# A gated cross-attention kernel of two layers: work moved across the layer boundary, Wffn's maximum in the third pass, O's scaling elsewhere in eight units

## What is computed

```python
x = x + tanh(g_xattn[0]) * L0_xattn(layernorm(x), ctx, Wq, Wk, Wv, Wo, q_norm_w, k_norm_w)   # 32 heads, 8 kv heads of 128, q and k rms-normed
x = x + tanh(g_ffn[0])   * L0_ffn(layernorm(x), weight)
x = x + tanh(g_xattn[1]) * L1_xattn(layernorm(x), ctx, Wq, Wk, Wv, Wo)                       # 16 heads, 4 kv heads of 96
x = x + tanh(g_ffn[1])   * L1_ffn(layernorm(x), A, B, Wr, br)

def L0_ffn(x, weight):                       # weight is Wffn, 1024 x 1024
    x_scale = 448.0 / max(max(abs(x)), 1e-12)
    w_scale = 448.0 / max(max(abs(weight)), 1e-12)
    return clip(x * x_scale, -448, 448) @ clip(weight * w_scale, -448, 448) / (x_scale * w_scale)
```

## Time and profile before

| | before |
|---|---|
| median of 3 executions | 2707.05 us (2704.16 to 2710.39) |
| the profiled execution | 2703.99 us |
| its span | 2702.2 us |
| PE busy | 2629.9 us, 97% |
| DVE busy | 1530.5 us, 57% |
| ACT busy | 1290.0 us, 48% |
| POOL busy | 1040.8 us, 39% |
| mean granted TensorE clock | 0.993 of full speed |

### The profile page before, as it was taken

How to read it: one execution, slowest core, us unless ns; L and a number is a source line. 1 busy time by engine, 2 the same in 40 slices (tenths; PEclk the granted TensorE clock), 3 DMA queues, 4 the chain that set the end, 5 groups by cost and what they waited for, 6 DMA issues and landing times. The chain is left out here.

```text
span 2702.2 us, 38854 instructions
## 1 busy us (share of the span) xinstructions
PE 2629.9 (97%) x13508; PEld 2242.5 (83%) x13508; DVE 1530.5 (57%) x2710; ACT 1290.0 (48%) x2846; POOL 1040.8 (39%) x882
## 2 busy tenths in 40 slices
PE   7999999999899999999999999999889999999998
PEld 6788778888898888877888888888788989788887
DVE  7767785444655333356656656665465311777776
ACT  6655664333444333366545555554252312755544
POOL 2555424576262111146555555555020000544430
PEclk9999999999999999999999999999999999999999
DMA  4566565465543323346333333332420232433311
GB/s 169 186 210 202 165 229 202 159 207 176 189 149 128 98 89 102 99 121 179 107 100 105 109 105 103 108 107 77 143 60 1 73 98 79 121 93 81 90 42 55
DMA packets 337897, 332.21 MB, mean 123 GB/s; under 512 B 127104, under 2 KB 275320, under 8 KB 337704
## 3 DMA queue, kind: packets, MB, share of 16 engines
q1 hardware_dynamic: 336616, 327.63, 38.9%
q10 hardware_dynamic: 1088, 2.10, 0.2%
HBM read 233.16 MB, written 96.49 MB: 122 GB/s over the span
## 5 line engine op out<-in xcount | busy, mean ns | idle before, releaser
L45 PE MATMUL pb<-p_ws,p_xs 128*128 128x512 f32 (+1 forms) x1124 | 436.4, 388 | 22.7 <-DVE p_xs L461 8.6
L47 PE MATMUL pb<-p_ws,p_xs 128*128 128x512 f32 (+1 forms) x1124 | 427.1, 380 | 0.0
L46 PE MATMUL pb<-p_ws,p_xs 128*128 128x512 f32 (+1 forms) x1124 | 426.2, 379 | 0.0
L823 POOL TENSOR_TENSOR p_xr<-p_xf 128x512 f32<-128x512 f32 x175 | 245.1, 1418 | 271.4 <-ACT p_xf L1019 162.5
L1692 ACT ACTIVATE at_p<-pb,at_nmax 112x487 f32<-112x487 f32 x256 | 171.5, 672 | 314.0 <-DVE at_nmax L1768 313.9
L1224 DVE TENSOR_TENSOR p_c<-pb,p_c 128x512 f32<-128x512 f32 (+1 forms) x280 | 175.6, 658 | 188.8 <-PE pb L47 188.0
L45 PEld LDWEIGHTS pb<-p_ws,p_xs 128*128 128x128 f32 x1124 | 212.5, 189 | 60.1 <-issue 15.3
L1530 POOL TENSOR_TENSOR at_k<-at_kr,at_k 128x488 fp32r<-128x488 f32 (+1 forms) x94 | 116.3, 1238 | 372.9 <-DVE at_k L1782 372.9
L47 PEld LDWEIGHTS pb<-p_ws,p_xs 128*128 128x128 f32 x1124 | 212.1, 189 | 36.4
L46 PEld LDWEIGHTS pb<-p_ws,p_xs 128*128 128x128 f32 x1124 | 212.7, 189 | 32.5
L1787 DVE TENSOR_TENSOR at_ptlo<-pb,at_pthi 125x448 fp32r<-125x448 f32 (+1 forms) x256 | 147.9, 620 | 80.5 <-ACT at_pthi L1714 80.3
(11 more groups left out here) (264 smaller groups left out, 6461.2 us busy)
## 6 DMA issues: line engine op xcount, KB each, us to landing
p_xf<-xT_d SPq DMA_DIRECT2D x23, 1024.0 KB, 5.6
p_raw<-in_L_xattn_Wq_dram SPq DMA_DIRECT2D x32, 512.0 KB, 4.2
at_raw<-in_L_xattn_Wo_dram SPq DMA_DIRECT2D x64, 256.0 KB, 2.7
xT_d<-p_xf SPq DMA_DIRECT2D x15, 1024.0 KB, 5.1
qT_d<-p_qstage SPq DMA_DIRECT2D x56, 256.0 KB, 2.7
at_qr<-qT_d SPq DMA_DIRECT2D x64, 224.0 KB, 3.1
at_rb<-rT_d SPq DMA_DIRECT2D x64, 224.0 KB, 3.4
at_kr<-kT_d SPq DMA_DIRECT2D x64, 187.5 KB, 2.9
```

The source lines that it names most:

```text
L45: pe.matmul(out, stat_hi, mov_hi, start=start, stop=False)
L46: pe.matmul(out, stat_hi, mov_lo, start=False, stop=False)
L47: return pe.matmul(out, stat_lo, mov_hi, start=False, stop=stop)
L823: pool.tensor_tensor(xr[:, n % 10, 1, :, :], src[:, a[0], HK * a[1]:HK * a[1] + HK, :], src[:, b[0], HK * b[1]:HK * b[1] + HK, :], op).the ...
```

## The change

- **Layer boundary.** `w1`, the high and low parts of layer 1's weights, and the semaphores of the cuts are allocated ahead of both layers. During layer 0's last 14 pieces ACT and POOL cut context tile 0, the eight key slabs and context tile 1; the loads are issued tile, key block, tile, value block, tile. The middle's list begins with the value slabs.
- **Wffn's maximum.** The eight blocks are read in the third pass as well, into `raw` (four behind pair 2's last product, four behind pair 3's); DVE takes a maximum in each of eight slots of pairs 3 and 4 (WM), and the one number is made in pair 4's last slot (WX), with POOL's reduction across partitions in it. `load_w(0)` to `(3)` move from pair 3's end to pair 5's second product. In the middle WM and WS are gone, WC starts at tile 1, and the low parts of Wffn are made by DVE, not POOL. T(0) and K(6) stand ahead of the first F.
- **Passes.** The load of pair 2's tiles, in passes 1 and 2, is issued at the end of the pass before, ahead of the last weight blocks, and no longer at pair 1's first XH. In passes 1 and 2 the second product of a direct pair takes the two halves in the other order.
- **Attention 0.** In units 1 to 8 (`unhurried`) DVE scales the previous unit's output behind the last two lows, and ACT and POOL cut it in the unit after. `oh` and `ol` lie interleaved.

The diff, cut:

```diff
+                    put(2, 3 + k // 4, 1 + k % 4, "WM", k)
+                put(2, 4, 6, "WX")
...
-                            for job in (7, 8):
-                                wait_low_v(sp, 2, job, HK - 1)
+                            sp.wait_ge(wf_topped, KS)
...
+                    def load_wf(k):
+                        if k >= 4:
+                            sp.wait_ge(wf_topped, k - 3)
+                        sp.dma_start(raw[:, k % 4, :, :].rearrange("p a n -> p (a n)"), wffn0[k * P:(k + 1) * P, :]).then_inc(wf_read[k % 4], 16)
...
+                            if j == 6:
+                                load_xf(w, 2)
...
-                                load_xf(w, p + 1)
+                                if p != 1:
+                                    load_xf(w, p + 1)
...
+                        if e[0] == "E" and e[1:] == (2, 2, 6):
+                            for job in (7, 8):
+                                wait_low_v(sp, 2, job, HK - 1)
+                            for k in range(4):
+                                load_wf(k)
                         if e[0] == "E" and e[1:] == (2, 3, 6):
+                            for k in range(4, KS):
+                                load_wf(k)
+                        if e[0] == "E" and e[1:] == (2, 5, 1):
                             for m in range(4):
                                 load_w(m)
...
-                    for c in range(2):
-                        sp.dma_start(w1_raw[:, c], w1T_d[c].rearrange("k p n -> p k n")).then_inc(w1_loaded[c], 16)
                     for i in range(3):
                         sp.dma_start(xc_raw[:, i, 1, :, :], xT_d[2 * NP1 - 1 + i]).then_inc(xc_loaded[i], 16)
+                        if i < 2:
+                            sp.dma_start(w1_raw[:, i], w1T_d[i].rearrange("k p n -> p k n")).then_inc(w1_loaded[i], 16)
...
+                        elif e[0] == "WX":
+                            pool.wait_ge(wf_most, 1)
+                            pool.partition_all_reduce(most[:], most[:], P, bass.bass_isa.ReduceOp.max).then_inc(wf_reduced, 1)
...
+                    for i in range(2):
+                        pool.wait_ge(xc_hi, i + 1)
+                        pool.tensor_tensor(xc[:, i, 1, :, :], xc_raw[:, i, 1, :, :], f32(xc[:, i, 0, :, :]), ALU.subtract).then_inc(xc_lo, 1)
+                        for k in range(KS if i == 0 else 0):
+                            pool.wait_ge(w1_hi, k + 1)
+                            pool.tensor_tensor(w1[:, 0, 1, k, :], w1_raw[:, 0, k, :], f32(w1[:, 0, 0, k, :]), ALU.subtract).then_inc(w1_lo, 1)
...
-                            for h in range(2):
+                            turns = (1, 0) if w and c else (0, 1)
+                            for h in turns:
...
+                    for i in range(2):
+                        act.wait_ge(xc_loaded[i], 16)
+                        act.activation(xc[:, i, 0, :, :], xc_raw[:, i, 1, :, :], ACT.Copy).then_inc(xc_hi, 1)
+                        if i == 0:
+                            act.wait_ge(w1_loaded[0], 16)
+                            act.wait_ge(att.projected, att.tail)
+                        for k in range(KS if i == 0 else 0):
+                            act.activation(w1[:, 0, 0, k, :], w1_raw[:, 0, k, :], ACT.Copy).then_inc(w1_hi, 1)
...
+                        elif e[0] == "WM":
+                            k = e[1]
+                            dve.wait_ge(wf_read[k % 4], 16 * (k // 4) + 16)
+                            dve.tensor_reduce(w_tops[:, k:k + 1], raw[:, k % 4, :, :].rearrange("p a n -> p (a n)"), AX.X, ALU.max,
+                                              apply_absolute_value=True).then_inc(wf_topped, 1)
+                        elif e[0] == "WX":
+                            w_scale()
...
-            oh = [place(f"oh{i}", [P, NK, TOKENS], F32R) for i in range(2)]
-            ol = [place(f"ol{i}", [P, NK, TOKENS], F32R) for i in range(2)]
+            oh, ol = zip(*((place(f"oh{i}", [P, NK, TOKENS], F32R), place(f"ol{i}", [P, NK, TOKENS], F32R)) for i in range(2)))
...
+            def unhurried(u):
+
+                return 1 <= u <= NB and not flip
...
+                    if unhurried(u - 1):
+                        cut_o(u - 2)
                     if u + 1 < U:
                         cut_v(u + 1)
-                    if u:
+                    if u and not unhurried(u):
                         cut_o(u - 1)
...
+                    if unhurried(u - 1):
+                        cut_o(u - 2)
...
-                    if u:
+                    if u and not unhurried(u):
                         take_o(u - 1)
                     if flip and u % NB in SLAB_AT:
                         cut_slab(slabs_by(u))
                     low(u, 2)
                     low(u, 3)
+                    if unhurried(u):
+                        take_o(u - 1)
...
-                yield ("C", 0)
-                for k in range(KS):
-                    yield ("W", k)
-                yield ("K", 0)
                 for k in range(KS):
                     yield ("W", KS + k)
-                yield ("C", 1)
+                yield ("K", 0)
                 yield ("V", 0)
                 yield ("A", 0)
                 yield ("B", 0)
                 yield from cut_next(0)
-                ahead = {1: [("A", 1), ("WM", 0), ("WM", 1), ("WM", 2), ("WM", 3)],
-                         2: [("WM", 4), ("WM", 5), ("WM", 6), ("WM", 7), ("WS", 0)],
-                         3: [("WC", 0), ("WC", 1), ("WC", 2)],
-                         4: [("WC", 3), ("WC", 4), ("WC", 5), ("S", 0)],
-                         5: [("WC", 6), ("WC", 7), ("S", 1), ("T", 0)]}
+                ahead = {1: [("A", 1), ("WC", 0)],
+                         2: [("WC", 1), ("WC", 2)],
+                         3: [("WC", 3), ("WC", 4)],
+                         4: [("S", 0), ("WC", 5), ("WC", 6)],
+                         5: [("WC", 7), ("S", 1)]}
                 for i in range(1, NX - 1):
                     yield ("K", i)
                     yield from ahead[i]
                     yield ("V", i)
                     yield ("B", i)
                     yield from cut_next(i)
+                yield ("T", 0)
+                yield ("K", NX - 1)
                 for t in range(TT):
                     yield ("F", t, 0)
                     yield ("A", t + 2)
...
-                yield ("K", NX - 1)
...
-                    pool.wait_ge(wf_most, 1)
-                    pool.partition_all_reduce(most[:], most[:], P, bass.bass_isa.ReduceOp.max).then_inc(wf_reduced, 1)
-                    for k in range(KS):
-                        pool.wait_ge(wf_hi_s, k + 1)
-                        pool.tensor_tensor(wf_lo[:, k, :], wf[:, k, :], f32(wf_hi[:, k, :]), ALU.subtract).then_inc(wf_lo_s, 1)
...
                     def scale_w(k):
+                        act.wait_ge(wf_loaded[k // 2], 32)
...
+                            for m in ([k - 1] if k else []) + ([k] if k == KS - 1 else []):
+                                dve.wait_ge(wf_hi_s, m + 1)
+                                dve.tensor_tensor(wf_lo[:, m, :], wf[:, m, :], f32(wf_hi[:, m, :]), ALU.subtract).then_inc(wf_lo_s, 1)
```

More of the change, by code:

```diff
@@ L121, in flamingo @@
         brb = sb(stack, "brb", [P, 8])
+        w_tops = sb(stack, "w_tops", [P, KS])
+        most, w_scl, back = (sb(stack, n, [P, 1]) for n in ("most", "w_scl", "back"))
+        LIMIT = 448.0
         def first_layer():
@@ L186, in first_layer @@
             w1_turned, w1_staged = sem("p0_w1turn"), sem("p0_w1staged")
+            wf_read = [sem(f"p0_wfr{i}") for i in range(4)]
+            wf_topped, wf_most, wf_reduced, wf_chain = (sem(f"p0_wf{n}") for n in ("top", "most", "red", "chain"))
             bg_summed, padded, xt_stored = sem("p0_bgsum"), sem("p0_pad"), sem("p0_xtst")
@@ L346, in events @@
                             put(2, p, m, "K2", p, c)
+                for k in range(KS):
+                    put(2, 3 + k // 4, 1 + k % 4, "WM", k)
+                put(2, 4, 6, "WX")
                 for k in range(KS):
@@ L1855, in vector @@
                         yield
[L1856 removed]
+            return Engines(sync, gpsimd, tensor, scalar, vector, o_taken, added, projected, PIECES * (NG - 1))
         def second_layer():
@@ L1931, in second_layer @@
             t_done, t_hi, t_lo = (sem(f"mid_{n}") for n in ("tdone", "thi", "tlo"))
-            wf_topped, wf_most, wf_reduced, wf_chain, wf_scaled, wf_clipped, wf_hi_s, wf_lo_s = (
-                sem(f"mid_wf{n}") for n in ("top", "most", "red", "chain", "scaled", "clipped", "hi", "lo"))
+            wf_scaled, wf_clipped, wf_hi_s, wf_lo_s = (sem(f"mid_wf{n}") for n in ("scaled", "clipped", "hi", "lo"))
             factored, f_done, f_added = (sem(f"mid_{n}") for n in ("fac", "fdone", "fadd"))
```

61 lines of the change are left out of this document (23 added, 38 removed).

## The result

| | median | ratio to before, 95% interval |
|---|---|---|
| before | 2704.9 us (2703.95 to 2710.39, 5 runs) | |
| changed | 2693.4 us (2693.0 to 2696.85, 5 runs) | 0.9962 (0.9951 to 0.9973) |

What follows compares the result with a forecast made beforehand. PE, busy 97% of the span, was taken as the bound. Gains of 15.0, 4.3 and 0.8 less losses of 1.8 and 9.1 made 9.2 us off the 2707.05 us median: 2697.9 us, range 2686.5 to 2704.5.

Steps and rivals of the forecast that it cites:

- Middle: Layer boundary to the Wffn product: of 19.3 us lost to PE waits and half clock, 15.0 us gained (13 to 17).
- The small wait at values(2): In the middle: one PE wait of 0.1 to 1 us remains, behind ACT's late values(1) copy.
- the net on DVE is zero: In the middle: DVE loses the reduces (2 x 4.59 us) but gains splitting of 8 x 1.14 us.
- Third pass, its start: Earlier context tile load starts POOL at 713.6; PE waits of 2.33 and 2.20 us go; 4.3 us gained (2.3 to 5).
- the turned halves: Third pass's start: PE begins 2.2 us earlier, but the next product waits for a split reached no sooner; zero gain.
- Pass 1's start: Early load of pair 2's tiles in the kernel's second pass: no PE wait follows the late load, so nothing gained.
- Eight maxima: Eight reduces of 1.15 us moved into the third pass delay DVE's adds, 0.9 us per pair; 1.8 us lost (0.5 to 3).
- Reduction: Third pass, POOL's reduction across partitions: code changes before and after idle PE 7.5 us, plus 1.6 half clock; 9.1 us lost (0 to 11).
- The change ahead of the reduction: POOL's code change before the reduction in pair 4's last slot: 7.1 us, ending at 783.2.
- rival 2: POOL's reduction, third pass: only the change back costs; PE idle 5.5 us plus 1.4; kernel at 2695.7 us; chance 0.17.
- The change back: POOL's code change from the reduction to elementwise instructions: 7.1 us, ending at 790.7, first sum at 792.0.
- O: Attention 0, output scaled later: a free unit takes 8.1 us, late units get slack; 0.8 us gained (-3 to 3).

## Why the prediction was right, and where it was not

**Middle** (15.0 forecast, 15.9 measured). The waits came out to 0.4 us: 11.8 us of idle gone (14.4 less 2.63) against the 11.4 forecast. One stretch at half clock was expected to stay and did, losing 1.7 us, not 1.4. Together 15.0; the remaining 0.9 us are what a wait costs beyond its bracket. PE in pair 3 of the changed kernel, matmul by matmul:

```profile
756.03 0.33 PE L46 MATMUL pb<-p_ws,p_xs 128*128 128x384 f32 x1
756.20 0.34 PE L47 MATMUL pb<-p_ws,p_xs 128*128 128x384 f32 x1
756.89 0.41 PE L45 MATMUL pb<-p_ws,p_xs 128*128 128x384 f32 x1 [0.34 <-DVE p_c L1266]
757.14 0.33 PE L46 MATMUL pb<-p_ws,p_xs 128*128 128x384 f32 x1
```

Undisturbed, one starts 0.17 us after the other and takes 0.33; across the wait of 0.34 us the starts are 0.69 us apart, and the next follows after 0.25. So a wait costs the bracket and about 0.25 us more, and the middle has four fewer. The small wait at values(2) didn't come.

The prediction put both later waits down to the chain behind the maximum. In DVE's queue one scaling of a row tile stands ahead of the splits that release the Wffn product. Before and after:

```profile
2006.43 2.94 DVE L2501 TENSOR_SCALAR mid_xn<-mid_xn 128x1024 f32<-128x1024 f32 x1
...
2005.33 0.69 DVE L2554 TENSOR_SCALAR mid_xn<-mid_xn 128x1024 f32<-128x1024 f32 x1 [1.16 <-ACT mid_xn L2454]
```

Before, it ran beside POOL's low parts of Wffn and took 2.94 us; in the changed kernel POOL is idle there, and it takes 0.69. The one ahead of the first transposes took 2.15 us before. That moving the low parts to DVE would shorten DVE's other instructions was not in the sum ("the net on DVE is zero"). How the 6.9 us divide between the maxima gone, the low parts moved and the order is not shown: only the order was run alone.

**Third pass, its start** (4.3, 4.6). POOL started at 714.54, forecast 713.6, and both waits went. That the turned halves bring nothing is what the run without them shows. No run takes back this early load alone, so its gain rests on POOL's start and the two waits in the trace.

**Pass 1's start** (0, 2.1 lost). This is the step that failed. I wrote of the early load that "in pass 2 no PE wait follows the same late load, so nothing is gained", meaning the kernel's second pass, and stopped there: I asked what POOL's earlier start would release, and not what runs beside it. It now runs beside DVE's four low parts, for which PE waits, and they take 5.75 us and not 2.49. The page of before had the hint:

```profile
L461 DVE TENSOR_TENSOR p_xs<-p_xr,p_xs 128x512 fp32r<-128x512 f32 x175 | 164.7, 966 | 26.0 <-ACT p_xs L1037 26.0
```

The mean for that line of DVE is 966 ns, over half as long again as the 0.62 us of one that runs alone.

**Eight maxima** (1.8, 2.7). The mechanism was right, and so was the idle time: 0.34 and 0.53 us in each pair, 0.9 together. The term was sized by idle time alone; with what the two waits cost beyond their brackets it is 1.3 us per pair by the distance.

**Reduction** (9.1, 8.3). Right in the place, the engine and the releaser; two terms off in opposite directions. The change ahead of the reduction was put at 7.1 us and would have ended at 783.2. It takes 5.5 us and was over as DVE's maximum arrived, to 0.1 us: covered, so that it cost nothing, as in rival 2. The change back was taken as 7.1 us from the middle and took 8.50. So the wait was 6.05 us and not 7.5, and the half clock cost 2.1 and not 1.6. So the size was nearly the forecast's and the mechanism rival 2's, which had 6.9 us for it with a change back 1.4 us shorter than it proved. That the sum came near is luck: a step too many against a step too short. The GPSIMD Engine Reference of the Trainium skill (Instruction dispatch) gives about 6 us for loading code; the steps measured here are 5.5 us to the reduction, 10.0 to 12.0 beside full DMA queues, and 6.9 to 9.0 back, each time that the kind of instruction changes.

**O** (0.8, 1.0). The unit of 8.0 us was forecast as 8.1. That the sum came out so near is chance, given how far its runs spread.

**Drift.** +0.5 us in pass 0 and -1.5 at the end belong to nothing that was changed: the last is mostly one stretch at half clock of 3.4 us where it was 6.8.

## What to carry to other kernels

A step moved to an engine that idles must be priced with what runs beside it, not only with what waits for it: an engine that starts earlier can slow its neighbour. A reduction across partitions among elementwise instructions on POOL belongs where POOL has 20 us of idle time on both sides together, and a small reduce on a tight engine belongs in the slots where that engine is idle, which its timeline shows one by one. And where two waits follow each other, take the second one's bound too before a gain is promised: removing 2.7 us ahead of the second gained 0.8.

## What the runs showed of the hardware

- POOL's step from elementwise instructions to the reduction across partitions took 5.5 us beside light transfers and 10.0 to 12.0 us in the four kernels where it stood beside full DMA queues; the step back 6.9 to 9.0 us in thirteen kernels. A second reduction right behind the first cost 0.5 us.
- A DVE subtraction of 128 x 512 with both inputs in SBUF takes 0.62 us alone and 1.44 us beside POOL's sums. A DVE TENSOR_SCALAR of 128 x 1024 took 0.69 us, and 2.15 to 2.94 beside POOL's subtractions of such tiles.
- A wait on PE costs about 0.25 us beyond the idle time in its bracket: matmuls of 0.33 us that follow each other start 0.17 us apart, across a wait of 0.34 us 0.69.
- Whether a stretch at half clock follows a wait of PE differs between executions. Behind 3.1 to 3.3 us at pass 1's start there was one in seven of eight profiled executions, behind 1.07 to 1.34 us in none of six; behind 2.4 us at the third pass's start in three of eleven; behind 2.6 us at the barrier in eleven of thirteen; behind 6.05 to 7.40 us in pair 5 in all seven, for 6.8 us or more.
